# Second attention: value parts made by VectorE in groups of four chunks, and folds cut into pieces between mask steps

## The reference

```python
support = (inputs @ weight).reshape(-1, H, D).transpose(1, 0, 2)
f1, f2 = ...                                   # one number per node and head, each
scores = leaky_relu(f1 + f2, 0.2)              # H x N x N
mask = scores * adj != 0
e = where(mask, exp(scores - m), 0)            # m: row maximum
attn = e / e.sum(axis=2)
out = einsum('hnm,hmd->hnd', attn, support)
x = x + out + bias + inputs @ proj_w.T + proj_b
```

## Time and profile before

| what | us |
|---|---|
| median of 3 runs | 2019.82 (2018.22 to 2021.35) |
| profiled execution, its own time | 2017.3 |
| span of the profile (first to last instruction) | 2015.4 |
| second attention, PE's matmuls, first start to last end | 939.2 to 1482.1 |
| PE busy there | 479.0 of 542.9 |
| DVE busy there | 349.6 |
| ACT busy there | 424.4 |
| POOL busy there | 143.0 |

### The profile page before, as it was taken

The page is one execution under the profiler, slowest core; times in us unless marked ns, Lnnn a source line. Parts: engine busy times, 40 slices in busy tenths (PEclk is TensorE's granted clock), DMA queues, the critical chain, the costliest instruction groups (busy, mean ns, idle before and its releaser), DMA issues. The chain is left out here.

```text
span 2015.4 us, 43515 instructions
## 1 busy us (share of the span) xinstructions
PE 1665.5 (83%) x12926; PEld 1536.0 (76%) x12927; DVE 980.1 (49%) x2116; ACT 1033.3 (51%) x2127; POOL 497.2 (25%) x558
## 2 busy tenths in 40 slices
PE   4649999994589997473897997979965899999998
PEld 3538888883579997353896897879965799999997
DVE  4638788885712222665765766756666111111111
ACT  1634444443245554114886787877843354545453
POOL 1100000000056765007605307200000233333332
PEclk9969999995689999696998999999975899999999
DMA  9960000003367776400000000000044566666664
GB/s 148 108 129 8 16 8 8 21 0 110 110 186 203 204 203 149 156 13 6 11 8 17 16 4 23 10 14 14 11 152 152 186 182 178 180 181 181 180 182 108
DMA packets 81365, 190.04 MB, mean 94 GB/s; under 512 B 9562, under 2 KB 52854, under 8 KB 72470
## 3 DMA queue, kind: packets, MB, share of 16 engines
q1 hardware_dynamic: 48438, 138.73, 21.0%
q0 software_dynamic: 27280, 45.56, 14.2%
q10 hardware_dynamic: 5584, 4.99, 0.8%
HBM read 189.37 MB, written 33.11 MB: 110 GB/s over the span
## 5 line engine op out<-in xcount | busy, mean ns | idle before, releaser
L1213 PE MATMUL bank<-arena 128*128 128x195 bf16 x5408 | 479.0, 249 | 104.8 <-DVE arena L1114 44.3
L1213 PEld LDWEIGHTS bank<-arena 128*128 128x128 fp8e4 x5408 | 467.6, 98 | 116.2 <-issue 114.6
L1024 ACT ACTIVATE arena<-arena,m_row 128x512 fp8e5<-128x512 f32 (+1 forms) x728 | 431.8, 677 | 132.8 <-DVE arena L1114 120.5
L1667 PEld LDWEIGHTS bank<-X,arena 128*128 128x128 f32 x2832 | 337.8, 194 | 6.5 <-DMA arena<-m0w 0.5
L1667 PE MATMUL bank<-X,arena 128*128 128x128 f32 x2832 | 338.2, 277 | 0.1
L1705 PE MATMUL bank<-arena,X 128*128 x1416 | 329.2, 383 | 4.6 <-ACT X L1740 4.4
L1764 DVE TENSOR_TENSOR arena<-bank,X 128x256 f32<-128x256 f32 x118 | 50.1, 425 | 559.0 <-PE bank L1705 552.3
L884 PE MATMUL bank<-arena 128*128 (+1 forms) x1352 | 299.6, 383 | 15.5 <-DVE arena L827 15.5
L884 PEld LDWEIGHTS bank<-arena 128*128 128x128 f32 x1352 | 257.1, 191 | 57.2 <-issue 21.4
L1705 PEld LDWEIGHTS bank<-arena,X 128*128 128x128 f32 x1416 | 260.8, 191 | 42.0 <-issue 11.0
L805 ACT ACTIVATE bank<-arena,s_all 128x384 f32<-128x384 f32 (+1 forms) x234 | 134.0, 573 | 183.8 <-DVE arena L819 175.8
(11 more groups left out here) (208 smaller groups left out, 1434.5 us busy)
## 6 DMA issues: line engine op xcount, KB each, us to landing
arena<-m1w SPq DMA_DIRECT2D x67, 1024.0 KB, 12.0
arena<-m0w SPq DMA_DIRECT2D x67, 512.0 KB, 8.0
arena<-adjT POOLq DMA_DIRECT2D x26, 416.0 KB, 12.8
xs<-X SPq DMA_DIRECT2D x4, 1664.0 KB, 6.9
arena<-qd SPq DMA_DIRECT2D x25, 256.0 KB, 3.2
xe<-zeros POOLq DMA_DIRECT2D x1, 3456.0 KB, 14.5
X<-x_in SPq DMA_DIRECT2D x2, 1664.0 KB, 11.2
xd<-X SPq DMA_DIRECT2D x13, 256.0 KB, 2.1
```

The costliest lines, as they stand in the source:

```text
L1024: last = a.activation(self.sign[slot].bitcast(F8W)[:, q * W:q * W + nt * P], self.row[r][:, 0:nt * P], ACT.Sigmoid, scale=STEEP, bias=self ...
L1213: last = pe.matmul(bank[r * NT + n][:, kind * KW:(kind + 1) * KW], self.split[slot][kind].bitcast(F8)[:, q * W + n * P:q * W + (n + 1) * P ...
L1667: last = pe.matmul(bank[2 * s + c // 4][:, c % 4 * P:(c % 4 + 1) * P], self.W1[s][:, k * HID + c * P:k * HID + (c + 1) * P], self.rxt[s][: ...
```

## The change

POOL no longer makes parts. DVE makes them, four chunks at a time (`tensor_copy` and `tensor_tensor` over 520 columns where they had 260), with one scratch buffer and one semaphore that counts groups; PE waits for the group of its step in place of the whole head. For head 0, group 0 stands ahead of the first mask step and the other six behind one mask step of block 0 each; group 0 of head 1 closes that block. After that block k of head h carries group k of head h+1, in four pieces; the last head carries none. The fold of the finished block is cut into pieces too. The DVE program is written out for each head, where it looped over pairs of heads.

```diff
-                tw = 2 * 2 * self.HC
-                self.scaled = [words(k + s * tw, tw) for s in range(2)]
-                k += 2 * tw
...
-            def scale(self, eng, who, h, slot, first, last, before):
...
-                HC, steps = self.HC, self.scale_steps[who]
...
-                with eng.Fori(first, last) as i:
-                    done = before + (i - first) * 5
...
-            def scale_gpsimd(self, pool):
-                n = PAIRS - self.FIRST
-                for h in range(self.H):
-                    if h == 0:
-                        pool.wait_ge(self.exp_ready, 2)
-                    if h >= 2:
-                        pool.wait_ge(self.parts_used[h % 2], h // 2)
-                    before = 0 if h == 0 else 5 * (n + (h - 1) * PAIRS)
-                    self.scale(pool, 0, h, h % 2, self.FIRST if h == 0 else 0, PAIRS, before)
-                    total = 5 * (n + h * PAIRS)
-                    pool.wait_ge(self.scale_steps[0], total)
-                    pool.sem_inc(self.parts_ready[h % 2], 1)
...
+            def part_scale(self, v, h, group, chunks):
...
+                c0, nth, f, out_ = self.part_views(h, group, chunks)
...
+                v.wait_ge(self.parts_ready, nth + 1)
+                for kind, e in enumerate((self.exp_sj, d_all)):
+                    last = v.tensor_tensor(f[:, kind, :, :], vals,
+                                           e[:, at(h * T + c0, chunks)].rearrange("p (c o) -> p c o", o=1)
+                                           .to_broadcast([P, chunks, self.HC]), ALU.mult)
+                last.then_inc(self.scale_steps, 1)
...
+            def part_round(self, v, h, group, chunks, g):
+
+                _, nth, f, out_ = self.part_views(h, group, chunks)
+                v.wait_ge(self.scale_steps, nth * 4 + 2 * g + 1)
+                v.tensor_copy(out_[:, :, :, g, :], f).then_inc(self.scale_steps, 1)
...
+            def part_rest(self, v, h, group, chunks):
...
+                _, nth, f, out_ = self.part_views(h, group, chunks)
+                v.wait_ge(self.scale_steps, nth * 4 + 2)
+                v.tensor_tensor(f, f, out_[:, :, :, 0, :], ALU.subtract).then_inc(self.scale_steps, 1)
...
+            def part_low(self, v, h, group, chunks):
...
+                v.wait_ge(self.scale_steps, nth * 4 + 4)
+                v.sem_inc(self.waited["dve"], 1)
+                v.tensor_tensor(out_[:, :, :, 2, :], f, out_[:, :, :, 1, :], ALU.subtract).then_inc(self.parts_ready, 1)
...
-                self.scale(v, 1, 0, 0, 0, self.FIRST, 0)
-                v.wait_ge(self.scale_steps[1], 5 * self.FIRST)
-                v.sem_inc(self.first_ready, 1)
+                self.scale_group(v, 0, 0, 4)
...
+                def fold_sum(first, last, h, k, j, r, nt):
+
+                    if first == 0:
+                        v.wait_ge(self.split_used[2], h * 7 + k + 2)
+                    for n in range(first, min(last, nt)):
+                        done = v.tensor_reduce(self.sums[:, n * 2 * HC:(n + 1) * 2 * HC]
                                                .rearrange("p (k x) -> p k x", k=2),
                                                bank[r * NT + n][:, 0:6 * HC]
                                                .rearrange("p (k g x) -> p k x g", k=2, g=3), AXX, ALU.add)
...
+                        if n == nt - 1:
+                            done.then_inc(st_, 1)
+                            v.wait_ge(st_, (h * 7 + k) * 7 + 1)
+                            v.sem_inc(self.bank_free[r], 1)
...
+                def first_block():
+
+                    for c in range(2):
+                        step(0, 0, 4 * c, 4, NT, c, 0, c, 0, c)
+                        self.scale_group(v, 0, 1 + c, 4)
+                    for c in range(2):
+                        step(0, 0, 8 + 4 * c, 4, NT, c, 1, c, 1, 2 + c)
+                        self.scale_group(v, 0, 3 + c, 4)
+                    for c in range(2):
+                        step(0, 0, 16 + 4 * c, 4, NT, c, 2, c, 2, 4 + c)
+                        self.scale_group(v, 0, 5 + c, 4 - 2 * c)
+                    step(0, 0, T - 2, 2, NT, 0, 3, 2, 0, 6)
+                    self.scale_group(v, 1, 0, 4)
...
-                    for s in range(2):
-                        step(b, k, 4 * s, 4, nt, s, b * (4 - s), s, b * 3, b * 7 + s)
-                    if earlier_block is not None:
-                        add_parts(*earlier_block)
-                    for s in range(2):
-                        step(b, k, 8 + 4 * s, 4, nt, s, b * (4 - s) + 1, s, b * 3 + 1, b * 7 + 2 + s)
-                    if earlier_block is not None:
-                        add_output(*earlier_block)
-                    for s in range(2):
-                        step(b, k, 16 + 4 * s, 4, nt, s, b * (4 - s) + 2, s, b * 3 + 2, b * 7 + 4 + s)
+                    part = (v, h + 1, k, 4 if nt == NT else 2) if h + 1 < H else None
+                    step(b, k, 0, 4, nt, 0, b * 4, 0, b * 3, b * 7)
+                    step(b, k, 4, 4, nt, 1, b * 3, 1, b * 3, b * 7 + 1)
+                    fold_sum(0, 2, *earlier)
+                    step(b, k, 8, 4, nt, 0, b * 4 + 1, 0, b * 3 + 1, b * 7 + 2)
+                    fold_sum(2, 4, *earlier)
+                    fold_scale(*earlier)
...
+                    step(b, k, 12, 4, nt, 1, b * 3 + 1, 1, b * 3 + 1, b * 7 + 3)
+                    fold_kinds(*earlier)
+                    if part:
+                        self.part_scale(*part)
+                    fold_den(*earlier)
+                    step(b, k, 16, 4, nt, 0, b * 4 + 2, 0, b * 3 + 2, b * 7 + 4)
+                    fold_inverse(*earlier)
+                    if part:
+                        self.part_round(*part, 0)
+                    fold_norm(*earlier)
+                    step(b, k, 20, 4, nt, 1, b * 3 + 2, 1, b * 3 + 2, b * 7 + 5)
+                    if part:
+                        self.part_rest(*part)
+                    fold_out(*earlier)
                     step(b, k, T - 2, 2, nt, 0, b * 4 + 3, 2, b, b * 7 + 6)
...
-                with v.Fori(0, H // 2) as hp:
-                    for p in range(2):
...
-                        block_(h, 0, NT, (h - 1, *tail) if p == 1 else None)
-                        with v.Fori(0, 2) as j:
...
-                        if p == 1:
-                            add_parts(h, *tail)
-                            add_output(h, *tail)
+                    if part:
+                        self.part_round(*part, 1)
+                        self.part_low(*part)
+
+                for h in range(H):
+                    tail = (6, 3, 0, NT // 2)
+                    if h == 0:
+                        first_block()
+                    else:
+                        block_(h, 0, NT, (h - 1, *tail))
+                    with v.Fori(0, 2) as j:
+                        block_(h, 2 * j + 1, NT, (h, 2 * j, j, 0, NT))
+                        block_(h, 2 * j + 2, NT, (h, 2 * j + 1, j, 1, NT))
+                    block_(h, 5, NT, (h, 4, 2, 0, NT))
+                    block_(h, 6, NT // 2, (h, 5, 2, 1, NT))
+                fold(H - 1, *tail)
...
-                pe.wait_ge(self.first_ready, 1)
...
-                            pe.wait_ge(self.parts_ready[p], hp + 1)
...
+                                pe.wait_ge(self.parts_ready, h * 7 + st + 2)
...
-                        pe.wait_ge(self.split_used[2], h * 7 + 8)
-                        pe.sem_inc(self.parts_used[p], 1)
...
-            @block.gpsimd
-            def _(pool):
-                with pool.If(pool.value_load(is_far[0:1, 0:1], min_val=0, max_val=1) < 1):
-                    Q1.scale_gpsimd(pool)
```

More of the change, by code:

```diff
@@ L962, in __init__ @@
                 self.row_steps = sem(tag + "row_steps")
[L963 to L966 removed]
+                self.scale_steps = sem(tag + "scale_steps")
+                self.parts_ready = sem(tag + "parts_ready")
                 self.row_loaded = [sem(f"{tag}row_loaded{r}") for r in range(2)]
@@ new lines, in part_low, with scale_group @@
+            def part_low(self, v, h, group, chunks):
+                _, nth, f, out_ = self.part_views(h, group, chunks)
+                v.wait_ge(self.scale_steps, nth * 4 + 4)
+                v.sem_inc(self.waited["dve"], 1)
+                v.tensor_tensor(out_[:, :, :, 2, :], f, out_[:, :, :, 1, :], ALU.subtract).then_inc(self.parts_ready, 1)
+            def scale_group(self, v, h, group, chunks):
+                self.part_scale(v, h, group, chunks)
+                self.part_round(v, h, group, chunks, 0)
+                self.part_rest(v, h, group, chunks)
+                self.part_round(v, h, group, chunks, 1)
+                self.part_low(v, h, group, chunks)
@@ L1115, in step, with sums4 @@
                                            op1=ALU.bitwise_and).then_inc(self.neg_ready[slot], 1)
-                def add_parts(h, k, j, r, nt):
-                    base = (h * 7 + k) * 7
-                    st = self.fold_steps
```

(33 more changed lines are left out.)

80 lines of the change are left out of this document (30 added, 50 removed).

## The result

| | us, median (runs) | ratio to before |
|---|---|---|
| before | 2020.07 (2018.22 to 2021.35) | |
| after | 1985.72 (1984.03 to 1988.47) | 0.983, 95% interval 0.9814 to 0.9846 |

The change makes the kernel 34 us faster; 20 were forecast, and the lowest time that the prediction reached, for its rival A, was 1991. The profiled execution of after took 1985.19 us (span 1983.5) against 2017.3 (span 2015.4): 32.1 us to account for.

What follows compares the result with a forecast made beforehand. PE was taken to be kept idle by the late start, DVE beside POOL, and waits in blocks and between heads. Terms -13.4 - 1.4 + 0.0 - 1.1 - 3.9 - 0.5 = -20.3, taken as -20: median 2000.0 us, range 1995 to 2006.

Steps and rivals of the forecast that it cites:

- rival A: Blocks carrying a group: the added pieces cost nothing, mask step 6 comes at 15.0 or earlier; 1991 us, chance 0.12.
- The block with a group: A block in which DVE also makes parts for the next head: forecast 19.25 us in place of 18.71.
- the stall: PE's wait inside a block: 0.79 us at mask step 2, forecast to move to the next block's step 0, growing by 0.54.
- B: Blocks carrying a group: DVE becomes their bound, 20.1 us per block; sum -5.5, 2014.5 us, chance 0.14.
- D: Kernel gets slower: blocks carrying a group exceed 20.4 us; at 20.9 us +8, 2028 us, chance 0.05.
- C: Head 0: PE stays at the low clock through block 0, block 1's first steps cold too; -14.5, 2005.5 us, chance 0.12.
- The start: Head 0, up to block 1's first mask step: DVE alternates mask steps and groups, so block 1 starts earlier; -13.4 us.
- a dependent one waits 0.18: Price of DVE instructions in a group: one needing the previous result starts 0.18 us later; a four-chunk group takes 3.65 us.
- The heads: Work inside heads: -1.4 for head 1, 0.0 for head 2, -1.1 for head 0 from block 1, 0 for head 3.
- Nothing: Terms counted as zero: PE's extra wait per step, the removed POOL list, and the jump of DVE's loop between heads 1 and 2.
- Between heads: Half-width last block: less fold ahead of its last sign, next row's load 1.3 us earlier; three times, -3.9, plus -0.5 at the end.
- so it was hidden: Jump of DVE's loop between heads 1 and 2: removing it gains nothing, since PE's gap there, 8.6 us, is the shortest.

Runs made afterwards that it cites:

- the two-pass loops: Kernel after with head 0's groups 1 and 2 in one DVE loop of two passes, 3 and 4 in another, so addresses come from a register: 1990.2 us.

## Why the prediction was too small

**Right.** The block with a group: 19.25 forecast, 19.20 measured; the stall went from step 2 to the next step 0, at 1.3 forecast and 1.25 measured; its cause was D6, as the version with two pieces moved shows. Mask instructions at 684 ns. Three rivals are out: the pieces do cost (A, 8.4 us), DVE doesn't bound the blocks (B), nothing got slower (D). For C, PE began block 0 at 1.2 GHz (granted clock 0.50) and had nearly 2.4 GHz (0.98) from 920.3 on, although it was busy for only 13.6 of those 21.7 us. So block 0 did not stay at the low level; but C's other half, that the first steps of block 1 run at it, came all the same, after the wait of 2.87 us, and cost 1.5 us. It was less than the 5.5 us that C as a whole was priced at. The thin-M case of the Trainium skill (TensorE: Matmul & The Clock Gate, part 1) has waits longer than its bursts; block 0 has bursts of 2.9 us with waits of 0.8 to 1.5 between them, so I had carried it too far for block 0.

**The start, -13.4, was -17.6.** The step that failed is "a dependent one waits 0.18". The row was read rightly, but it belongs to an instruction in a loop with a register instruction in front. The changed code is written out, and waits 0.03 to 0.15. That makes a group 3.19 in place of 3.65, a cycle 4.40 in place of 4.86; from D0 to D5 and two more groups that is some 3 us. The rest, 1.2, was gained ahead of the stage and lies within what that point moves from kernel to kernel: luck, not mechanism.

**The heads, -2.5 with -3.9 between them and -0.5 at the end, were -13.5.** The forecast for them is -6.9. I cut each head at DVE's first mask step of block 1 and of block 6, the half-width one, and add up the heads (block 0 of head 0 left out):

| us | before | before, loop written out | after |
|---|---|---|---|
| PE's start to block 1, heads 1 to 3 | 57.4 | 55.7 | 56.6 |
| block 1 to block 6, four heads | 384.5 | 381.1 | 379.5 |
| block 6 to PE's last matmul, four heads | 54.8 | 53.9 | 47.0 |

Two steps failed. The first stands under "Nothing": that DVE's loop over head pairs matters only by its jump. I compared the old rows with the new program as if the same instruction had one price in both. Writing the loop out alone takes 3.4 us from blocks 1 to 5 and 0.9 from the half-width blocks; in head 3, where I wrote 0 and found -3.3, it takes 1.0 of the 1.7 that blocks 1 to 5 lost. One place where it shows is the scaling behind the reduces, in block 1 of head 3 before and written out:

```profile
1381.82 0.70 DVE L1134 TENSOR_TENSOR arena<-arena,q_cols 128x520 f32<-128x520 f32 x1 [0.70 <-DVE arena L1125]
```

```profile
1371.61 0.70 DVE L1134 TENSOR_TENSOR arena<-arena,q_cols 128x520 f32<-128x520 f32 x1 [0.27 <-DVE arena L1125]
```

The second is the term "Between heads": "2.37 us of fold stood ahead of it", "now ... about 1.1", so 1.3 three times and 0.5 at the end. Mask steps 0 and 4 of the half-width block of head 1, before and after:

```profile
1196.75 0.43 DVE L1112 SCALAR_TENSOR_TENSOR arena<-arena 128x256 uint32<-128x256 uint32 x1 [1.95 <-ACT arena L1024]
1206.01 0.42 DVE L1112 SCALAR_TENSOR_TENSOR arena<-arena 128x256 uint32<-128x256 uint32 x1 [0.32 <-DVE X L1157]
```

```profile
1173.75 0.42 DVE L1114 SCALAR_TENSOR_TENSOR arena<-arena 128x256 uint32<-128x256 uint32 x1 [0.65 <-ACT arena L1021]
1180.91 0.42 DVE L1114 SCALAR_TENSOR_TENSOR arena<-arena 128x256 uint32<-128x256 uint32 x1
```

Step 4 starts 9.26 us behind step 0 before and 7.16 after. I had counted only the fold between steps 3 and 4; the reduces cut in two bring step 3 forward as well, from 6.40 to 5.67. The half-width blocks lost 7.7 us in all where 4.4 were forecast, and in head 3 it was 1.7, not 0.5. The two kernels with POOL's parts show that the pieces do most of it: with whole folds these stretches add up to 53.8 us, in pieces to 48.0.

Writing the loop out takes 5.9 us from the heads, near the 6.6 that are missing, but the two don't lie in the same places, so the likeness is partly chance. And the first blocks of the heads, 1.7 of the 5.9, move by themselves. PE at the start of head 2, in the kernel after and in its second run:

```profile
1194.41 19.27 PE L1256 MATMUL bank<-arena 128*128 128x195 bf16 x208 [9.01 <-DVEq L1137]
```

```profile
1195.64 20.74 PE L1256 MATMUL bank<-arena 128*128 128x195 bf16 x208 [9.33 <-DVEq L1137]
```

In stretches of 2 us from there the granted clock is 0.50, 0.80 and 1.00 in the one and 0.50, 0.50 and 0.52 in the other; the same 208 matmuls differ by 1.5 us.

**The loop's jump, "so it was hidden", was not.** It cost 3.2 us. I had argued from the gap between heads 1 and 2 being the shortest of three (8.7). That gap was short for a different reason, the fold ahead of the masks, and would have been 5.6 without the jump. The change took the jump away (-3.1) and put the fold behind mask step 1 (+3.4): two errors of mine that cancelled in the time, by luck. Neither could be seen in the result alone.

What stays open: in which single instructions the 3.4 us of blocks 1 to 5 lie, whether the 3.2 us at the jump are a fetch, and when after a wait PE starts at the low clock.

## What to carry to other kernels

When a change also turns a loop into straight code, count that as an edit of its own: a row of the old program with a register instruction in front of it has that in its price, and doesn't hold for the new one. When an engine waits between two phases, list every semaphore it needs at that point and where each stands in the other engine's order; the one named in the shortest gap may be hidden by another. And of work that must be done in a phase, put last what nobody waits for: moving two pieces behind the mask that gates the next block gave 25 us for no work saved.

## What the runs showed of the hardware

- In a group with fixed addresses a VectorE instruction starts 0.03 to 0.04 us behind the one that it waits for (0.15 at the last of the group, where a semaphore increment stands between); in the two-pass loops, with a register instruction in front, 0.15 to 0.25. Independent ones start 0.07 to 0.09 before the last one's end.
- A short loop's jump on DVE cost 0.34 us (3.90 - 3.56) in one loop and 0.54 in the other, the jump back over two heads 3.2.
- PE kept a granted clock of 0.98 over 21.7 us in which it was busy for 13.6, with waits of 0.8 to 1.5 us between its bursts. After waits of 2.87 and 2.50 us it fell to 0.50; after waits of 2.49 and 3.23 us it did not, so the length of the wait alone doesn't tell.
- The rounding of 520 columns to bf16 takes 0.43 us (0.44 estimated), that of 260 0.30.
